# The last quad's third layer in two parts by samples, in an embedding-and-cross kernel on one core

## The reference

```python
for W in (f0, f1, f2):                        # 39*39, 128*39 and 128*39 rows by 128
    z = einsum('bfd,bgd->bfgd', x0, xk).reshape(b, f * g, d)
    cur = einsum('bpd,pm->bmd', z, W)
    outs.append(cur); xk = cur
z = sum(concatenate(outs, axis=1), axis=-1)   # over the 16 numbers: 1024 x 384
h = concatenate([z, dense_ctx], axis=1)       # 400 columns
h = maximum(h @ W_top1 + b_top1, 0)           # 512
h = maximum(h @ W_top2 + b_top2, 0)           # 256
y = h @ W_top3                                # 1
```

## Time and profile before

| | us |
|---|---|
| median of 3 runs | 1300.53 |
| these runs | 1299.10 to 1301.32 |
| the profiled execution, its own time | 1301.78 |
| its span, first to last instruction | 1300.0 |

### The profile page before, as it was taken

One profiled execution on the slowest core, in us unless ns is written; L12 is line 12 of the kernel. 1 busy time (PEld: TensorE's weight loads), 2 busy tenths in 40 slices (PEclk: granted clock), 3 DMA queues, 4 the chain that ended last, 5 costly groups with the idle time before them and its releaser, 6 DMA issues. The chain is left out here.

```text
span 1300.0 us, 21778 instructions
## 1 busy us (share of the span) xinstructions
PE 1262.0 (97%) x5983; PEld 1024.4 (79%) x5983; DVE 1050.4 (81%) x3210; ACT 938.3 (72%) x3084; POOL 958.0 (74%) x743
## 2 busy tenths in 40 slices
PE   3799999999999999999999999999999999999998
PEld 2477778888788887888878888788878888788887
DVE  3498999788887888788887788968889788877873
ACT  2488788677776777677776778767777677777773
POOL 7588888678886778777886778867888678874461
PEclk9899999999999999999999999999999999999999
DMA  5573333332232333213333123333123333222000
GB/s 137 95 185 69 60 66 66 64 66 49 42 51 62 64 66 64 42 31 66 67 64 65 19 53 65 67 63 62 28 51 63 65 64 63 47 39 52 4 1 1
DMA packets 129501, 76.36 MB, mean 59 GB/s; under 512 B 90792, under 2 KB 98201, under 8 KB 129379
## 3 DMA queue, kind: packets, MB, share of 16 engines
q1 hardware_dynamic: 119139, 72.32, 27.1%
q0 software_dynamic: 10240, 2.64, 2.5%
HBM read 68.42 MB, written 3.87 MB: 56 GB/s over the span
## 5 line engine op out<-in xcount | busy, mean ns | idle before, releaser
L414 ACT ACTIVATE parts<-pieces,x_cols 128x128 f32<-128x128 f32 x2560 | 729.6, 374 | 270.1 <-PE pieces L723 219.7
L555 DVE SCALAR_TENSOR_TENSOR parts<-pieces,x_cols,parts 128x128 f32<-128x128 f32 x2432 | 685.3, 344 | 200.0 <-PE pieces L723 155.5
L721 PE MATMUL pieces<-w_hi,cur_hi 128*128 128x512 f32 (+1 forms) x1280 | 543.1, 424 | 7.3 <-issue 3.5
L723 PE MATMUL pieces<-w_hi,cur_lo 128*128 128x512 f32 (+1 forms) x1280 | 499.8, 391 | 0.0
L722 PE MATMUL pieces<-w_lo,cur_hi 128*128 128x512 f32 (+1 forms) x1280 | 499.3, 390 | 0.0
L363 POOL TENSOR_TENSOR parts<-parts 128x1024 f32<-128x1024 f32 x127 | 304.6, 2398 | 202.2 <-DVE parts L555 197.9
L354 POOL DMA_INDIRECT emb<-in_table,rows x320 | 312.3, 976 | 81.6 <-issue 66.2
L721 PEld LDWEIGHTS pieces<-w_hi,cur_hi 128*128 128x128 f32 x1280 | 241.8, 189 | 66.4 <-ACT parts L414 6.1
L722 PEld LDWEIGHTS pieces<-w_lo,cur_hi 128*128 128x128 f32 x1280 | 242.4, 189 | 50.4
L723 PEld LDWEIGHTS pieces<-w_hi,cur_lo 128*128 128x128 f32 x1280 | 241.2, 188 | 51.4
L368 POOL TENSOR_TENSOR tails<-parts 128x512 f32<-128x512 f32 x127 | 164.5, 1295 | 18.1
(11 more groups left out here) (78 smaller groups left out, 608.2 us busy)
## 6 DMA issues: line engine op xcount, KB each, us to landing
partners<-x_wide SPq DMA_DIRECT2D x62, 546.0 KB
partners<-x_wide SPq DMA_DIRECT2D x31, 468.0 KB
x_rep<-x_wide SPq DMA_DIRECT2D x96, 78.0 KB
emb<-in_table,rows POOLq DMA_INDIRECT x320
x_diag<-x_cols SPq DMA_DIRECT2D x256, 10.0 KB
x_wide<-emb SPq DMA_DIRECT2D x32, 80.0 KB
x_wide<-emb SPq DMA_DIRECT2D x32, 32.0 KB
wt<-in_wt SPq DMA_DIRECT2D x1, 1024.0 KB
```

The costliest lines, as they stand in the source:

```text
L414: last = nc.scalar.activation(parts[n % 2][:, 4 * i + r, :], src[:, r * H:(r + 1) * H], ACT.Copy, scale=x_cols[n // 4][:, n % 4, f:f + 1])
L555: nc.vector.scalar_tensor_tensor(acc, src[:, r * H:(r + 1) * H], x_cols[n // 4][:, n % 4, f:f + 1], acc, ALU.mult, ALU.add).then_inc(acc_d ...
L721: nc.tensor.matmul(dst[:, 0:width], hi[:, cols], w1_hi[:, ws], start=True, stop=False)
L723: nc.tensor.matmul(dst[:, 0:width], lo[:, cols], w1_hi[:, ws], start=False, stop=True).then_inc(l2d_ready if q in D_PIECES else l2a_ready, 1)
```

## The change

In the last quad the 39 matmuls of the third layer are no longer done at the end over all 128 samples. `layer3_part` does them twice: once over the samples of the first three tiles (96 columns) and once over those of the last tile (32 columns), into `x_bank` and not `cur1_bank`. The first part needs G of blocks 0 to 11 only and is spread out: fields 0 to 4, 5 to 13 and 14 to 26 stand where the 13 warm-up matmuls stood, ahead of the G products of blocks 13, 14 and 15, and fields 27 to 38 stand behind the last of these. The second part waits for the last copy into G.

The top of the last quad has its own code and semaphores: ScalarE copies sum2 as soon as G is whole; TensorE puts in sum2's four matmuls ahead of its wait for sum3; each of the four output groups signals by itself; ScalarE takes the relus of groups 0 and 2, VectorE those of 1 and 3 (a `tensor_scalar`, add and max); `top2` goes over the groups k outside and the two halves inside, the halves in two banks; ScalarE takes the first half's relu, VectorE the second's; `top3` waits for each.

```diff
--- before.py
+++ after.py
@@ -154,7 +154,7 @@
         x_turns = [gx_bank[:, X_AT + j * F:X_AT + (j + 1) * F] for j in range(4)]
         h_sums = [cur1_bank[:, m * P:(m + 1) * P] for m in range(N1 // P)]
         h1_last = [pieces[m][:, 0:P] for m in range(N1 // P)]
-        h2_last = [pairs[:, m * P:(m + 1) * P] for m in range(N2 // P)]
+        h2_last = [pairs[:, 0:P], gx_bank[:, 0:P]]
 
 
         w0_raw = partners[1][:, 0:2, :].rearrange("p j c -> p (j c)")[:, 0:PAIRK * H].rearrange(
@@ -219,6 +219,13 @@
         h1_copied = sem("h1_copied")
         h2_ready = sem("h2_ready")
         h2_copied = sem("h2_copied")
+        sum2_last = sem("sum2_last")
+        h1_last_ready = sem("h1_last_ready")
+        h1_last_act = sem("h1_last_act")
+        h1_last_dve = sem("h1_last_dve")
+        h2_last_ready = sem("h2_last_ready")
+        h2_last_act = sem("h2_last_act")
+        h2_last_dve = sem("h2_last_dve")
         y_ready = sem("y_ready")
         y_copied = sem("y_copied")
         out_stored = sem("out_stored")
@@ -531,10 +538,18 @@
             u = QUADS - 1
             for n in range(BLOCKS - G_LAG, BLOCKS):
                 copy_g(u, n)
-            copy_l3(u)
-            relu1(u, 0, h1_last)
-            relu1(u, 1, h1_last)
-            relu2(u, h2_last)
+            act.wait_ge(g_copied, QUADS * BLOCKS)
+            act.wait_ge(y_ready, u)
+            nc.scalar.activation(sum2.rearrange("p (t b) -> p t b", b=TILE_B), G[:, :, F, :], ACT.Copy
+                                 ).then_inc(sum2_last, 1)
+            act.wait_ge(l3_ready, u + 1)
+            nc.scalar.activation(sum3, x_bank[:, 0:P], ACT.Copy).then_inc(l3_copied, 1)
+            for m in (0, 2):
+                act.wait_ge(h1_last_ready, m + 1)
+                nc.scalar.activation(h1[:, m, :], h1_last[m], ACT.Relu, bias=bt1[:, m:m + 1]).then_inc(h1_last_act, 1)
+            act.wait_ge(h2_last_ready, 1)
+            act.wait_ge(h1_last_ready, N1 // P)
+            nc.scalar.activation(h2[:, 0, :], h2_last[0], ACT.Relu, bias=bt2[:, 0:1]).then_inc(h2_last_act, 1)
             copy_y(u)
 
 
@@ -663,6 +678,15 @@
             add_last_parts()
             halve_tails(QUADS - 1, BLOCKS - 1)
             finish_cur2(QUADS - 1, BLOCKS - 1)
+            dve.wait_ge(top_loaded, 7 * 16)
+            dve.wait_ge(h2_ready, QUADS - 1)
+            for m in (1, 3):
+                dve.wait_ge(h1_last_ready, m + 1)
+                nc.vector.tensor_scalar(h1[:, m, :], h1_last[m], bt1[:, m:m + 1], 0.0, ALU.add, ALU.max
+                                        ).then_inc(h1_last_dve, 1)
+            dve.wait_ge(h2_last_ready, 2)
+            nc.vector.tensor_scalar(h2[:, 1, :], h2_last[1], bt2[:, 1:2], 0.0, ALU.add, ALU.max
+                                    ).then_inc(h2_last_dve, 1)
 
 
         @block.tensor
@@ -783,6 +807,12 @@
                     last = nc.tensor.matmul(cur1_bank[0:1, 0:P], wt3[:, k:k + 1], h2[:, k, :], start=k == 0,
                                             stop=k == N2 // P - 1)
                 last.then_inc(y_ready, 1)
+
+            def layer3_part(tiles, cols, fields):
+
+                for f in fields:
+                    last = nc.tensor.matmul(x_bank[:, cols], w2[:, f, :], G[:, tiles, f, :], start=f == 0, stop=f == F - 1)
+                return last
 
             def warm_up(count, bank):
 
@@ -839,25 +869,42 @@
             u = QUADS - 1
             pe.wait_ge(cur1_lo_ready, QUADS * TILES)
             pe.wait_ge(sum1_ready, QUADS * TILES)
-            warm_up(4, x_bank)
+            most, rest = slice(0, TILES - 1), slice(TILES - 1, TILES)
+            most_cols, rest_cols = slice(0, (TILES - 1) * TILE_B), slice((TILES - 1) * TILE_B, P)
+            pe.wait_ge(g_copied, (u + 1) * BLOCKS - 4)
+            layer3_part(most, most_cols, range(0, 5))
             make_g(u, BLOCKS - 3)
-            warm_up(4, x_bank)
+            layer3_part(most, most_cols, range(5, 14))
             make_g(u, BLOCKS - 2)
             pe.wait_ge(acc_done, QUADS * BLOCKS * D_OPS)
             pe.wait_ge(prod_done, QUADS * BLOCKS * len(A_PIECES))
             for m in range(N1 // P):
                 top1_early(u, m, h1_last)
-            warm_up(5, x_bank)
+            layer3_part(most, most_cols, range(14, 27))
             make_g(u, BLOCKS - 1)
-            pe.wait_ge(y_copied, u)
-            for step in range(len(S_L3)):
-                layer3(u, step, QUADS * TILES)
+            layer3_part(most, most_cols, range(27, F))
+            pe.wait_ge(g_copied, (u + 1) * BLOCKS)
+            layer3_part(rest, rest_cols, range(0, F)).then_inc(l3_ready, 1)
+            pe.wait_ge(sum2_last, 1)
+            for m in range(N1 // P):
+                nc.tensor.matmul(h1_last[m], wt1[:, 1, m * P:(m + 1) * P], sum2, start=False, stop=False)
             pe.wait_ge(l3_copied, u + 1)
             for m in range(N1 // P):
-                top1_late(u, m, h1_last)
-            for m in range(N2 // P):
-                top2(u, m, h2_last)
-            top3(u)
+                nc.tensor.matmul(h1_last[m], wt1[:, 2, m * P:(m + 1) * P], sum3, start=False, stop=True
+                                 ).then_inc(h1_last_ready, 1)
+            for k in range(N1 // P):
+                pe.wait_ge((h1_last_act, h1_last_dve)[k % 2], k // 2 + 1)
+                for m in range(N2 // P):
+                    last = nc.tensor.matmul(h2_last[m], wt2[:, k, m * P:(m + 1) * P], h1[:, k, :],
+                                            start=k == 0, stop=k == N1 // P - 1)
+                    if k == N1 // P - 1:
+                        last.then_inc(h2_last_ready, 1)
+            pe.wait_ge(y_copied, u)
+            for k in range(N2 // P):
+                pe.wait_ge((h2_last_act, h2_last_dve)[k], 1)
+                last = nc.tensor.matmul(cur1_bank[0:1, 0:P], wt3[:, k:k + 1], h2[:, k, :], start=k == 0,
+                                        stop=k == N2 // P - 1)
+            last.then_inc(y_ready, 1)
 
 
 def kernel(**inputs):
```

## The result

The changed kernel takes 1308.86 us (median of four runs, 1306.84 to 1310.30); the kernel before takes 1299.82 in the same comparison. The ratio is 1.0068, 95% interval 1.0056 to 1.0081: **slower by 0.7%**, 9 us. The forecast was 1302.6, the range ended at 1304.8. The profiled execution took 1306.84, with a span of 1305.0.

What follows compares the result with a forecast made beforehand. The end was taken as one thread of TensorE and ScalarE steps waiting for each other. Layer three ending 4.94 us later, less 2.84 gained in the tail, gave +2.1 on 1300.53, so 1302.6; range 1293.5 to 1304.8.

Steps and rivals of the forecast that it cites:

- The first filler to block 15's G product: TensorE near the end: 27 matmuls over 96 columns replace 13 warm-ups, so this G product starts 3.08 us later.
- The 24 passes behind it: Behind block 15's G product: 12 matmuls over 96 columns, 2.70 us, cover the 0.84 us wait for G's copy.
- The price of a pass: Each float32 matmul is two passes; each costs its load of 128 weight columns, 0.1127 us, even with fewer moving columns.
- Rivals 1 and 1b: Layer three's short passes: 0.030 us by moving columns, 1293.8 (chance 0.17); or 0.061 as in the transposes, 1296.2 (0.08).
- The tail: From layer three's end to the start of the copy of y: 7.30 us becomes 4.46, a gain of 2.84.
- half of the last layer: In the tail: two of the last layer's four passes remain behind the last relu, a gain of 0.17 us.
- The waits hidden around the two later relus: In the tail, behind the second top layer: one of its two relus is hidden, a gain of 0.41 us.
- The sum at the full clock: Whole kernel, load-bound passes: layer three's +4.94 and the tail's -2.84 give +2.1 us, 1302.6; chance 0.66.
- rival 2: Layer three's short passes count as idleness; the clock halves midway through the 78, adding 8.5 us: 1311.1; chance 0.06.

Runs made afterwards that it cites:

- the tail alone: Changed kernel with the 13 warm-ups back and layer three done once over 128 columns behind the last copy into G, new tail kept: 1296.82 us, ratio 0.9976.
- the run with 128 columns: Changed kernel with the last 78 passes of layer three moving all 128 columns and not 32, nothing else different: 1302.25 us, ratio 1.0018.

## Why the prediction was wrong

*The first filler to block 15's G product*: right. 8.97 forecast, 8.87 measured in the changed kernel. The 24 passes behind it hid the copy into G, as forecast.

*The price of a pass*, on which the forecast was built: right, and now shown. With 128 weight columns, passes of 32, 64, 96 and 128 columns all take 0.112 from start to start (0.1127 in the sum), and with 64 weight columns one of 32 costs 0.059. Rivals 1 and 1b fall. The Trainium skill's figure for the load (TensorE: Matmul & The Clock Gate, LDWEIGHTS: 107 ns for 128 columns) agrees with the 109 ns read from the load records; the 25 ns of its section on the issue gap do not show here, where each matmul brings its own float32 weights.

*The tail*: nearly right, 2.84 forecast and 2.71 measured with the tail alone. The 0.17 for half of the last layer did not come: its four passes run in one piece of 0.60 us, as before, and all of them wait for the second top layer's first relu (1292.78, 0.33 behind the last pass). The waits hidden around the two later relus did come (0.41 forecast; from the last pass of the second top layer to the first of the last one 0.71 before, 0.32 to 0.33 after), but VectorE has no part in it: without it the time is the same.

*The sum at the full clock*: 2.10 forecast, 2.05 in the profile and 2.6 in the medians of the run with 128 columns. That it is so close is in part luck: layer three ended 4.76 later and not 4.94 (its passes took 0.112), the tail gained 2.71 and not 2.84, and the two errors cancel.

**The step that failed** is the one that took all passes of the last part at the full clock, and gave rival 2 a chance of 0.06. The prediction had the mechanism there, "only 30 of every 113 ns stream", a fall midway through the 78 passes, 8.5 us in price and 1311.1 as the time. What happened is that rival: the clock halves some 5 us into the short passes and comes back in the second top layer, where each pass streams 128 columns again. It cost 4.8 us in the profiled executions and 6.2 to 6.6 in the medians (1308.86 and 1308.48 against 1302.25). The rival's price of 8.5 was too high at both ends: in the short passes the low clock cost 23.55 - 20.98 = 2.6 and not 4.4, because it fell later than midway, and in the tail 6.85 - 4.59 = 2.3 and not 4.1, because it came back before the end. The argument against the rival was the mistake: that "the loads run without a gap here" was taken as work that keeps the clock. The run with 128 columns shows that the columns streamed decide it: loads, waits, order and count of instructions are the same there.

What stays open: in the changed kernel the profiled executions were the fastest of four both times (1306.84, 1306.60), and the others stand 2 us above them. Either they reached the first filler later (in the profiles it starts at 1271.5 to 1274.7), or the clock was down for longer (in the profiles with a fall, 10.2, 10.2 and 13.6 us). No trace shows which. Each run's mean granted clock is on record, 0.991 in all of these but the slowest (1310.30, with 0.989; 0.001 is 2.6 us at the half level). For that one it speaks for more time at the low level; for the others it decides nothing, since the mean also takes in stretches at 0.50 near the start of the kernel (about 38 to 45 and 52 to 58 us in the changed kernel's profile). Where between 32 and 64 columns the clock is lost was not tried, nor short passes with 64 weight columns in a longer run.

## What to carry to other kernels

A float32 matmul with weights of its own costs at least the load of its weight columns (here 0.11 us a pass for 128 of them); cutting its 128 moving columns into parts pays that cost once for each part and saves nothing. Filler that replaces warm-up work is not free merely because the engine was busy anyway: here 27 matmuls in place of 13 warm-ups moved the last G product by 3 us. And work that keeps TensorE "busy" mostly by loads can lose the clock for itself and for what follows it, so ask of each stretch how much of it streams.

## What had not been expected of the hardware

With 32 moving columns a pass of 112 ns, 78 in a row, the granted clock went to 0.50 in all three profiles that had them, 3.7 to 5.7 us behind their start, and stayed there for 10.2 to 13.6 us; with 64 columns (one profile) or 128 at the same pace it stayed at 1.00. The profile gives TensorE and its loads 2.00 of 2.00 us busy in the short passes, ahead of the fall and behind it.

VectorE's relu out of PSUM (128 x 128, add and max) takes 0.35 us and ScalarE's single one 0.37; in a run of four ScalarE needs 1.14 / 4 = 0.29 for each.
